# Softmax denominators moved from matrix products with ones to accumulated exponentials on ScalarE

## What is computed

```
x = LN(x + linear_attention_and_mlp(x))                       # no softmax
x = LN(x + windowed_cross_attention(x, ctx))                  # 16 heads, keys within 64 places
x = LN(x + six_cell_network(x))                               # each cell: attention of 8 heads
x = LN(x + causal_linear_attention(x))                        # no softmax
x = LN(x + masked_cross_attention(x, ctx, padding_mask))      # 16 heads
x = LN(x + fourier_linear(x))

def attention(q, k, v):                                       # in the 2nd, 3rd and 5th block
    scores = einsum('bqhd,bkhd->bhqk', q, k) * scale
    attn = softmax(scores, axis=-1)
    return einsum('bhqk,bkhd->bqhd', attn, v)
```

## Time and profile before

| | |
|---|---|
| median of 3 runs | 3996.06 us (3991.0 to 4010.05) |
| the profiled execution | 4006.72 us, of which the span of the trace is 4005.0 us |
| busy: PE, DVE, ACT, POOL | 3573.8, 1925.5, 1679.8, 947.2 us |
| mean granted clock of PE | 0.931 of full speed |

### The profile page before, as it was taken

The page is one execution under the profiler, slowest core; times in us unless marked ns, Lnnn a source line. Parts: engine busy times, 40 slices in busy tenths (PEclk is TensorE's granted clock), DMA queues, the critical chain, the costliest instruction groups (busy, mean ns, idle before and its releaser), DMA issues.

```text
span 4005.0 us, 82977 instructions
## 1 busy us (share of the span) xinstructions
PE 3573.8 (89%) x35084; PEld 2593.2 (65%) x35084; DVE 1925.5 (48%) x3647; ACT 1679.8 (42%) x3338; POOL 947.2 (24%) x763
## 2 busy tenths in 40 slices
PE   6989889989888989899998999989898998988986
PEld 5766667666656766666675666756666675666654
DVE  4453453564455535555354645535455353642423
ACT  1234444444434444344444444444344443444432
POOL 6460040142203204040220503104040220500000
PEclk8989999999999999999998998999899998999987
DMA  6000000000000000000000000000000000000000
GB/s 212 20 1 4 1 9 4 10 4 9 4 1 9 4 10 4 9 4 1 10 4 9 4 1 9 4 10 4 9 4 1 10 4 9 4 1 4 4 6 3
DMA packets 40731, 44.02 MB, mean 11 GB/s; under 512 B 4656, under 2 KB 40240, under 8 KB 40240
## 3 DMA queue, kind: packets, MB, share of 16 engines
q1 hardware_dynamic: 40368, 38.72, 3.1%
HBM read 34.52 MB, written 4.19 MB: 10 GB/s over the span
## 4 chain that ended last, share of the span: by engine, by line
PE 72%; DVE 11%; issue 6%; ACT 6%; POOL 4%; DMA 0%; SPq 0%; DVEq 0%; ACTq 0%; POOLq 0%
PE banks L664 17%; PE banks L656 13%; PE banks L870 12%; PE banks L838 9%; DVE nmx L1168 7%; PE banks L811 5%; ACT work L1377 4%; PE banks L776 3%; PE banks L649 3%; POOL work L1526 2%; PE banks L842 2%; PE banks L671 2%; PE banks L943 2%; PE banks L822 1%; POOL work L1516 1%
## 5 line engine op out<-in xcount | busy, mean ns | idle before, releaser
L1168 DVE TENSOR_REDUCE nmx<-banks 128x4 f32<-128x1024 f32 (+1 forms) x640 | 717.2, 1165 | 338.6 <-PE banks L811 337.7
L664 PE MATMUL banks<-work,weights 128*128 128x256 f32 x3584 | 843.5, 385 | 9.1 <-ACT work L1276 7.4
L1377 ACT ACTIVATE work<-banks 128x1024 f32<-128x1024 f32 (+1 forms) x640 | 602.4, 980 | 531.2 <-PE banks L842 530.9
L664 PEld LDWEIGHTS banks<-work,weights 128*128 128x128 f32 x3584 | 667.9, 191 | 146.9 <-issue 49.1
L656 PE MATMUL banks<-weights,work 128*128 128x256 f32 x2688 | 658.4, 392 | 18.4 <-ACT work L1304 8.4
L656 PEld LDWEIGHTS banks<-weights,work 128*128 128x128 f32 x2688 | 505.1, 194 | 122.7 <-issue 42.5
L838 PE MATMUL banks<-work 32*128 32x256 f32 (+1 forms) x5120 | 466.2, 451 | 83.2 <-DVE nmx L1168 23.6
L1526 POOL TENSOR_TENSOR work<-work 128x512 f32<-128x512 f32 x256 | 385.1, 1522 | 174.2 <-DVE work L1134 164.4
L811 PE MATMUL banks<-work 32*128 32x256 f32 (+1 forms) x5120 | 356.0, 397 | 69.4 <-ACT work L1377 21.5
L1181 DVE TENSOR_TENSOR work<-banks,work 128x256 f32<-128x256 f32 x256 | 108.3, 423 | 643.7 <-ACT work L1387 643.4
L1553 POOL TENSOR_TENSOR work<-work,row 128x512 f32<-128x512 f32 x64 | 82.3, 1286 | 1320.5 <-PE banks L649 1320.5
(11 more groups left out here) (151 smaller groups left out, 3683.9 us busy)
## 6 DMA issues: line engine op xcount, KB each, us to landing
work<-in_w_setup SPq DMA_DIRECT2D x41, 256.0 KB, 5.9
work<-in_ctx SPq DMA_DIRECT2D x32, 256.0 KB, 3.0
work<-in_x SPq DMA_DIRECT2D x16, 256.0 KB, 2.9
out<-work SPq DMA_DIRECT2D x16, 256.0 KB, 2.2
weights<-in_w_all SPq DMA_DIRECT2D x1, 3072.0 KB, 16.5
weights<-in_w_all SPq DMA_DIRECT2D x2, 1024.0 KB, 10.4
weights<-in_w_all SPq DMA_DIRECT2D x1, 2048.0 KB, 16.9
row<-in_rows SPq DMA_DIRECT2D x1, 1664.0 KB, 7.5
```

Source lines behind the costliest of these rows:

```text
L664: ins = e.matmul(b[:, m * 256:m * 256 + 256], wslot(w)[:, k, m * P:m * P + P], xin[:, k, :], start=(k == 0 and (m == 0 or closed)) if star ...
L1168: e.tensor_reduce(nmax(s, n)[:, 2 * p:2 * p + 2, :], b, AX, ALU.max, negate=True).then_inc(*freed("max", n, p, i))
L1377: e.activation(dst, src, ACT.Exp).then_inc(*freed("exp", n, p, i))
```

## The change

The sums no longer come from PE. After `max` has read a pair of banks, ACT runs four exponentials on it (`sum`, one for each of two row groups and two halves of the queries, 128 by 256 each, 192 for `x`), with the negated maximum as the bias of each partition. They write in place into PSUM, where nobody reads them, and their accumulated output goes to a small tile `sums`. Only then is the pair free. One logarithm of 128 by 8 (`ln_sum`) follows; DVE subtracts it from the negated maximum (a third small instruction in `split`), and maximum plus logarithm are what is transposed and subtracted in `st`. So the exponentials come out normalised, `pv` loses its products with ones, and `norm` becomes a DVE copy (for `y` a product with one number) with nothing on ACT.

The core of the diff (the waits that were added let quads of a pair run in either order; set-up lines of `ones` and `one_of` go):

```diff
@@ entry_steps, heads(n, q, k, v): the steps, their assumed us and what they free
-        maxed = [do("DVE", "s", (n, p), 1.13 if kind != "x" else 0.87, b, frees=((b, p),)) for p in range(2)]
-        maxed = [do("DVE", "split", n, 0.3, *maxed)]
+        maxed = [do("DVE", "s", (n, p), 1.16 if kind != "x" else 0.87, b) for p in range(2)]
+        summed = [do("ACT", "sum", (n, p), 1.4 if kind != "x" else 1.25, maxed[p], frees=((b, p),)) for p in range(2)]
+        maxed = [do("DVE", "split", n, 0.45, do("ACT", "ln_sum", n, 0.2, *summed))]
...
-        r = do("ACT", "norm", n, 0.6, pv, kept)
-        return do("DVE", "norm", n, 0.4, r, frees=((opened, 3),))
+        return do("DVE", "norm", n, 0.4, pv, kept, frees=((opened, 3),))
@@ tensor(e), op "pv"
-                    for what in range(2):
-                        for kc in range(NC):
-                            for g in range(4):
-                                left = (v[:, kc, 128 * f + 32 * g:128 * f + 32 * g + 32] if what == 0
-                                        else one_of[:, par, :] if par is not None else ones[:, 0:32])
...
+                    for kc in range(NC):
+                        for g in range(4):
...
@@ vector(e), op "split"
-                    for p in range(2):
-                        e.wait_ge(*when("max", a, p, i))
+                    e.wait_ge(*when("log sums", a, i))
+                    e.tensor_tensor(nmax(s, a, 0), nmax(s, a, 0), t["sums"][:, a % 2], ALU.subtract).then_inc(
+                        *tell(vec[s], "shifts", a, i))
+                    e.wait_ge(*when("shifts", a, i))
@@ vector(e), op "norm"
-                    e.tensor_tensor(ctx_out(s, a), at("norm", a, i)[:, 0:S], ctx_out(s, a), ALU.mult).then_inc(
-                        *freed("norm", a, i))
+                    e.wait_ge(*when("pv mm", a, i))
...
+                        ins = e.tensor_copy(ctx_out(s, a), at("norm", a, i)[:, 0:S])
@@ scalar(e)
-                elif op == "norm":
...
+                elif op == "sum":
+                    n, p = a
+                    use(EXP_SET)
+                    e.wait_ge(*when("maxima", n, p, i))
+                    w = SPAN if quad(n)[0] == "x" else S
+                    for j in range(2):
+                        for c in range(NC):
+                            b = at("max", n, p, i)[:, j, c * 256:c * 256 + w]
+                            ins = e.activation(b, b, ACT.Exp, bias=nmax(s, n)[:, 2 * p + j, c:c + 1],
+                                               accum_out=t["sums"][:, n % 2, 2 * p + j, c:c + 1])
+                    ins.then_inc(*freed("max", n, p, i))
+                elif op == "ln_sum":
+                    use(EXP_SET)
+                    for p in range(2):
+                        e.wait_ge(*when("max", a, p, i))
+                    e.activation(t["sums"][:, a % 2], t["sums"][:, a % 2], ACT.Ln).then_inc(
                         *tell(act[s], "log sums", a, i))
```

More of the change, by code:

```diff
@@ L860, in tensor @@
                     half = half_of[i, a]
-                    for what in range(2):
-                        for kc in range(NC):
-                            for g in range(4):
-                                left = (v[:, kc, 128 * f + 32 * g:128 * f + 32 * g + 32] if what == 0
-                                        else one_of[:, par, :] if par is not None else ones[:, 0:32])
[L866 to L874, removed]
+                    for kc in range(NC):
+                        for g in range(4):
+                            qq = queries(kind, kc)
+                            cut = SPAN if kind == "x" and kc and first else qq.stop
+                            for lo, hi in ((qq.start, cut), (cut, qq.stop))[:1 + (cut < qq.stop)]:
+                                ins = e.matmul(b[32 * g:32 * g + 32, lo:hi],
+                                               v[:, kc, 128 * f + 32 * g:128 * f + 32 * g + 32],
+                                               pt(half, g)[:, 0, kc * 256 + lo - qq.start:kc * 256 + hi - qq.start],
+                                               start=(first and kc == 0), stop=(last and kc == NC - 1),
+                                               tile_position=(0, 32 * g))
                     ins.then_inc(*tell(pe[s], "pv mm", a, i))
@@ L1178, in vector @@
                 elif op == "norm":
-                    e.wait_ge(*when("inverse sums", a, i))
-                    kind, c, f, par = quad(a)
-                    e.tensor_tensor(ctx_out(s, a), at("norm", a, i)[:, 0:S], ctx_out(s, a), ALU.mult).then_inc(
-                        *freed("norm", a, i))
+                    e.wait_ge(*when("pv mm", a, i))
+                    if quad(a)[0] == "y":
+                        e.wait_ge(*when("one if kept", i))
+                        ins = e.tensor_scalar(ctx_out(s, a), at("norm", a, i)[:, 0:S], t["kept"][:, 2:3], None, ALU.mult)
+                    else:
+                        ins = e.tensor_copy(ctx_out(s, a), at("norm", a, i)[:, 0:S])
+                    ins.then_inc(*freed("norm", a, i))
                 elif op == "co" and a == NODES - 1:
@@ L1377, in scalar @@
                     e.activation(dst, src, ACT.Exp).then_inc(*freed("exp", n, p, i))
-                elif op == "norm":
-                    kind, c, f, par = quad(a)
+                elif op == "sum":
+                    n, p = a
                     use(EXP_SET)
-                    e.wait_ge(*when("pv mm", a, i))
-                    e.activation(ctx_out(s, a), at("norm", a, i)[:, S:2 * S], ACT.Ln).then_inc(
-                        *tell(act[s], "log sums", a, i))
-                    e.wait_ge(*when("log sums", a, i))
-                    if kind == "y":
-                        e.wait_ge(*when("minus kept", i))
-                    e.activation(ctx_out(s, a), ctx_out(s, a), ACT.Exp,
-                                 scale=t["kept"][:, 2:3] if kind == "y" else -1.0).then_inc(
-                        *tell(act[s], "inverse sums", a, i))
+                    e.wait_ge(*when("maxima", n, p, i))
[11 more added lines that the diff above has]
+                    e.activation(t["sums"][:, a % 2], t["sums"][:, a % 2], ACT.Ln).then_inc(
+                        *tell(act[s], "log sums", a, i))
                 elif op in ("cq", "ck"):
```

36 lines of the change are left out of this document (16 added, 20 removed).

## The result

The changed kernel takes 4388.06 us (median of 4 runs, 4385.88 to 4396.38) beside 3993.53 us for the kernel before on the same chip: a ratio of 1.098, 95% interval 1.095 to 1.102, slower. The forecast was 4076 us, the range ended at 4300. The direction was right, the size was a fifth of what came.

What follows compares the result with a forecast made beforehand. The prediction took the kernel as close to bound by PE's work (busy 89%). From the profiled 4006.7 us, -289 + 291 + 77 gave 4086, less 10.7 to the median: 4076 us; own range 4030 to 4180, 8-in-10 range 3815 to 4300.

Steps and rivals of the forecast that it cites:

- the waits: 112 pairs by 2.6 us: PE waiting for banks and `nm` behind ACT's sums: 2.6 us more at 112 quad pairs, +291 us, bounds 80 and 416.
- the clock: PE's granted clock falls after new waits: one more fall of 4.8 us a period, +77 us, bounds 0 and 230.
- The ones: Products with ones removed from PE: 269 us at full clock, -289 at the mean clock, gained in full.
- The prediction's own place: PE at the fifth cell, quads 13 and 12: waits of 2.2 and 2.6 us, together 4.8 us for one pair.
- rival A: PE's work decides, latency hidden: 3807 us, or 3707 us by the rule of the most-contended engine alone; chance 0.31.
- Rival C: ACT's accumulated output has its own price, 0.58 us more a group, 258 us in all: 4334 us; chance 0.13.
- ACT's time: ACT's busy time with the sums added and `norm` shortened: 2543 us, 64% of the span, which fits.
- `norm` and `split`: `norm` on ACT shortened, taken as 0, at most 20 us; `split` on DVE 61 us longer, hidden.
- rival B: Gain and loss cancel, with 200 us of new waits and 75 of clock: 3982 to 4010 us; chance 0.12.

Runs made afterwards that it cites:

- experiment 1: Kernel before, in its own order, without the products with ones and ACT's `norm` (context not normalised): 3858.52 us, ratio 0.964.
- experiment 5: Changed kernel with pair of banks free after its maximum, sums run on SBUF, `split` and `nm` waiting for the maxima only: 4458.08 us, ratio 1.113.
- experiment 6: Changed kernel with both waits for the sums gone and the sums queued behind their quad's `exp`, taken last of what is ready: 4030.64 us, ratio 1.006.
- experiment 7: Changed kernel with all its waits, but one exponential in each group of sums instead of four: 4068.47 us, ratio 1.016.
- experiment 2: Changed kernel without the accumulated output of its exponentials, the logarithm made a copy of constants: 4241.38 us, ratio 1.059.
- experiment 3: Changed kernel with pair of banks free after its maximum, exponentials working on SBUF, `split` still waiting for the sums: 4489.9 us, ratio 1.121.
- experiment 4: Changed kernel with sums still holding the pair, but `split` and `nm` going after the maxima, sums unused: 4381.37 us, ratio 1.095.
- experiment 9: Changed kernel with the planner's durations for sums, logarithm and split set to those of the trace: 4397.9 us, ratio 1.099.
- experiment 10: Changed kernel with the products with ones put back on PE, their result unused: 4592.23 us, ratio 1.147.

## Why the prediction was wrong, point by point

**The step that failed is the waits: 112 pairs by 2.6 us.** It gave +291 us with +77 for the clock, 368 together. Measured, from the kernel of experiment 1 to the change, it is 530 us. With the ones, of which 140 us came instead of 289, that makes up the 312 us between forecast and time: some 160 from here and 149 from there. The prediction's own place came out near (4.3 us against 4.8, in part by luck, as its three waits show), but one place was taken for all. It counted what a quad's own pair of banks and its own `nm` wait for. It did not count that ACT's list is shared: sums of one entry stand ahead of copies, `exp` and the release of banks of another, as in the 7.31 us above. Experiments 5, 6 and 7 show that this is the mechanism and not a side of it: with both waits for the sums gone the loss stays, with the sums further back in the list 427 us of it go, and the other lists alone can't account for it. How the 530 us split between the hold, the link and the queue was not told apart. The prediction's remark that the copy "stands on ACT behind the eight exponentials of quad 12" had the mechanism, and then priced it at one place.

**The ones: -289 us in full.** The work was sized right: 269 us at full clock explain PE's busy time in experiment 1 (3573.8 - 269 = 3304.8, measured 3311.6). What failed is "the gain in full if nothing else moves". Only 140 us reached the span; PE's idle time took 117. A share of 72% on the chain didn't mean that each microsecond of it was worth one. The Trainium skill ("Perfetto Trace Analysis", Identifying Performance Opportunities) says that improving a kernel generally means improving its most-contended engine. It gives no size; rival A's 3707 us took the 289 us in full. With PE relieved and nothing put in, the time is 3859 us, 140 us less: experiment 1 agrees with the rule in sign.

**The accumulated output.** Rival C had the mechanism and not the size. A read of its own follows each exponential, and a group takes 1.80 us, not the 2.2 that was to prove C. Its time, 4334 us, lay nearest to what came, but by luck: it had 258 us for the accumulated output, and the reads cost 147. With the measured 0.36 us of reads in a group its own working (112 pairs by four groups) gives 161. The rest of the loss is not C's.

**ACT's time** was forecast at 2543 us and is 2655; read from starts, the group of four is 15% longer than was taken. It fits, and that was no comfort: 60% busy says nothing of who stands behind whom.

**The clock.** +77 us and 0.91 were forecast; 0.871 and 197 us came. In experiment 1, with more idle time but few waits over 3 us (14, 71 us), the clock stayed at 0.934; in the change, with 66 of them (346 us), it fell. Behind the wait of 7.31 us the granted clock was 0.50 from 2243.4 to 2250.0 us, its lower level. That the long waits bring the whole fall is a reading of these numbers and was not tried by itself. The period of an entry is 262.8 us against 244 forecast, from two stores in a row of SP's timeline:

```profile
2140.49 0.38 SPq L1604 DMA_DIRECT2D out<-work  x1
...
2403.33 0.38 SPq L1604 DMA_DIRECT2D out<-work  x1
```

The last entry, alone, has a clock of 0.74.

**`norm` and `split`.** Taken as 0 and hidden. `norm` on ACT was left out together with the ones in experiment 1, so its part isn't told apart. The third instruction of `split` came to 79 us of DVE where 61 were taken; it stays in experiments 2 to 7, 9 and 10, so its own price isn't told apart either. That `split` waits for the sums was taken away in experiment 4, with no effect.

**Rivals A and B** needed idle time below 500 us, or 200 us of new waits; idle is 892.8. The range left out what came. Even with the upper bounds of both terms, 416 us of waits and 230 of clock, its sum gives 4353 us at most: the bound of the waits was made of the same single place (160 pairs by 2.6), with no term for one entry's sums in another entry's way. The range was also narrow for its own chances: it began above rival A's 3807 us and ended below C's 4334, though the two held 0.44.

Two readings of the prediction are slightly off, and neither matters to the result. The projection was taken at 1.73 us, where the earlier trace rows have 1.98 from start to start; and 2914 us of ACT are 67% of 4334, not 68%.

## What to carry to other kernels

Work that is moved to a half-idle engine is priced by who stands behind it in that engine's list, not by that engine's load: list for each new instruction what is queued after it, of other entries too, and who waits for that. Test it by removing the waits and keeping the work; if the loss stays and goes when the work stands further back, it is the queue. And before work is moved off the bounding engine, ask whether it can be made cheaper in place: here that gave -4.4%, at the price of coarser sums, where moving it gave +9.8%.

## What the runs showed of the hardware

- ACT's accumulated output adds an ACTIVATION_READ_ACCUMULATOR to each ACTIVATE, 235 ns by its record, 0.09 us by the pitch in a full queue.
- An exponential of 128 by 256 from PSUM to PSUM in place has a pitch of 0.36 us to its read; from SBUF to SBUF in bfloat16 it is 0.40 (2277.12 to 2277.52 us in experiment 5):

```profile
2277.12 0.49 ACT L1391 ACTIVATE trash<-row,eps 128x256 bf16<-128x256 f32 x1
2277.52 0.19 ACT L1391 ACTIVATION_READ_ACCUMULATOR trash<-row,eps 128x1 f32 x1
2277.61 0.49 ACT L1391 ACTIVATE trash<-row,eps 128x256 bf16<-128x256 f32 x1
```

- In a run of sixteen exponentials with their reads the records grow from 0.45 to 0.53 us, while their starts stay 0.45 us apart: the length of a queued record is not its cost.
- Eight bfloat16 products with 32 columns of output weights and 256 moving columns, in four column groups, take 0.37 us, 43% of the same in fp32.
